# Top-16 cross-attention of a two-layer transformer kernel: its negation moved from GpSimd to ScalarE, one cycle for each tile, scores in four PSUM banks, and the work on tokens at fixed places of the cycle

## What is computed

```
scores = jnp.einsum('bqhd,bkhd->bhqk', q, k) / jnp.sqrt(jnp.float32(D)).astype(h.dtype)
top_s, top_i = jax.lax.top_k(scores, TOPK)
attn = jax.nn.softmax(top_s, axis=-1)
...
o = jnp.einsum('bhqk,bhqkd->bqhd', attn, vg).reshape(B, L, C)
```

## Time and profile before

| | us |
|---|---|
| median of 3 runs (1690.25 to 1695.0) | 1692.53 |
| the profiled execution, its own time | 1693.09 |
| span of its profile | 1691.3 |
| busy in the span: PE / DVE / ACT / POOL | 1469.3 / 917.7 / 694.0 / 385.8 |
| attention 2 in the profile, from the first scores to the last output copy | 207 to 652 |

### The profile page before, as it was taken

One profiled execution on the slowest core, in us unless ns is written; L12 is line 12 of the kernel. 1 busy time (PEld: TensorE's weight loads), 2 busy tenths in 40 slices (PEclk: granted clock), 3 DMA queues, 4 the chain that ended last, 5 costly groups with the idle time before them and its releaser, 6 DMA issues.

```text
span 1691.3 us, 25766 instructions
## 1 busy us (share of the span) xinstructions
PE 1469.3 (87%) x9132; PEld 742.6 (44%) x9132; DVE 917.7 (54%) x2815; ACT 694.0 (41%) x1370; POOL 385.8 (23%) x632
## 2 busy tenths in 40 slices
PE   5999767788887786889899889998999998998898
PEld 3567544454644553343233223333323245453565
DVE  2555467777777766644356655665657335450111
ACT  2255433444344342313435435554455753334211
POOL 0020077775776754000000010000100001010110
PEclk9999967789889887889999989999999999999999
DMA  5022100000000001000010000000000000000000
GB/s 170 1 82 77 49 1 14 7 1 1 4 2 1 27 1 34 0 1 0 1 63 1 1 1 1 1 2 1 1 10 1 1 2 2 11 2 4 14 16 25
DMA packets 22095, 26.77 MB, mean 16 GB/s; under 512 B 4204, under 2 KB 19634, under 8 KB 21708
## 3 DMA queue, kind: packets, MB, share of 16 engines
q1 hardware_dynamic: 21059, 25.03, 4.6%
q10 hardware_dynamic: 909, 0.10, 0.0%
HBM read 21.58 MB, written 3.08 MB: 15 GB/s over the span
## 4 chain that ended last, share of the span: by engine, by line
PE 53%; DVE 6%; ACT 3%; issue 2%; POOL 1%; ACTq 0%; DVEq 0%; POOLq 0%
PE bank L863 24%; PE bank L820 7%; PE bank L901 7%; PE bank L835 5%; PE bank L799 3%; DVE part_max L1294 2%; PE bank L778 2%; PE bank L904 1%; PE bank L906 1%; ACT pr L1087 1%; PE bank L757 1%; DVE x_hat L1267 1%; PE bank L785 1%; ACT h_t L1029 1%; PE bank L764 1%
## 5 line engine op out<-in xcount | busy, mean ns | idle before, releaser
L1087 ACT ACTIVATE pr<-bank 128x512 f32<-128x512 f32 x656 | 355.0, 597 | 440.5 <-PE bank L863 440.5
L1294 DVE TENSOR_REDUCE part_max<-bank 128x1 f32<-128x512 f32 x512 | 328.3, 685 | 269.1 <-PE bank L863 268.2
L863 PE MATMUL bank<-slot 32*128 32x512 f32 (+1 forms) x3072 | 413.2, 530 | 7.8 <-ACT pr L1087 2.8
L863 PEld LDWEIGHTS bank<-slot 32*128 32x128 f32 x3072 | 164.0, 188 | 222.7 <-issue 158.6
L1344 POOL TENSOR_SCALAR var_eps<-mean_var 128x4 f32<-128x4 f32 x24 | 5.4, 227 | 1081.5 <-DVE mean_var L1258 1081.3
L820 PE MATMUL bank<-h_t,w_m 128*128 128x512 f32 x256 | 134.3, 653 | 13.3 <-DVE hidden L1274 7.8
L1104 ACT ACTIVATE exp_all<-bank,neg 128x154 f32<-128x154 f32 x256 | 85.3, 388 | 147.1 <-POOL neg L1389 143.8
L1403 POOL TENSOR_SCALAR left<-left 128x308 f32<-128x308 f32 x128 | 126.1, 985 | 75.7 <-issue 48.4
L901 PE MATMUL bank<-pr,v 128*17 128x512 f32 x1024 | 138.0, 612 | 0.0
L1319 DVE MAX8 top<-bank 128x8 f32<-128x154 f32 x256 | 69.6, 314 | 68.5 <-PE bank L925 65.3
L1406 POOL TENSOR_TENSOR probs<-left,exp_all 128x256 f32<-128x256 f32 x128 | 93.4, 730 | 0.0
(11 more groups left out here) (140 smaller groups left out, 1949.2 us busy)
## 6 DMA issues: line engine op xcount, KB each, us to landing
w_m<-in_L_xcond_w_m SPq DMA_DIRECT2D x1, 2048.0 KB, 9.5
w_m<-in_L_xcond_w_m SPq DMA_DIRECT2D x2, 1024.0 KB, 6.4
w<-in_L_xcond_w SPq DMA_DIRECT2D x2, 1024.0 KB, 6.7
w_ada<-in_L_xcond_w_ada SPq DMA_DIRECT2D x1, 1792.0 KB, 10.2
x_sb<-in_x SPq DMA_DIRECT2D x6, 256.0 KB, 6.7
res_row<-rows_dram SPq DMA_DIRECT2D x12, 128.0 KB, 3.3
out_x<-x_sb SPq DMA_DIRECT2D x6, 256.0 KB, 2.1
wa<-in_L_xcond_w_qkv SPq DMA_DIRECT2D x1, 768.0 KB, 7.3
```

Source lines behind the costliest of these rows:

```text
L863: last = nc.tensor.matmul(g.bank(*tile)[:, into], left, right, start=True, stop=True)
L1087: nc.scalar.activation(m.pr[:, u % NPR, :], g.bank("s", gi, i)[:, :], ACT.Exp).then_inc(g.free("s", gi, i), 1)
L1294: nc.vector.tensor_reduce(m.part_max[:, slot, h * TB + i // 8, i // 4 % 2:i // 4 % 2 + 1], bank[:, :], axis=AX.X, op=ALU.max).then_inc(don ...
```

## The change

Four things are changed, all within attention 2.

1. `c_neg` is issued by ScalarE, as an activation Copy with scale -1.0, and no longer by GpSimd. Its waits stay the same.
2. `topk_run` plans in a cycle of 5.2 us per tile. The scores of a tile are placed about a cycle ahead and rotate over the banks 1, 2, 3, 4. The transposes of a tile stand later, half a cycle into the next tile, and `c_copy` and `c_pv` follow.
3. The dense steps stand at fixed places: once a cycle at 0.35 for stage (2, 1), and at 0.10 and 0.60 of a cycle for (3, 0) and (4, 0), through `under` and `fill`; those that follow on DVE are planned 0.4 of a cycle later. The slots of `gap_slots` put an ACT follow-up right behind its PE step (`ua`, `ua_copy`), and the `silu` of batch 0 come in twos. `joined` lays the head of a block over the tail of the one ahead. The 16 + 45.5 cycles hold the same steps as before.
4. Banks of the dense steps and of `o_turn` of attention 2 are 0 and 6 (bank 6 is shared with `c_tail`; bank 0 is taken first where it is empty), no longer 0 and 1.

The plan of attention 3 begins 0.3 cycles (1.6 us) after the end of attention 2, where it was 3.5 half-tile steps (9.1 us). The number of matmuls, DVE and POOL operations is otherwise the same. The activation tables are loaded for `silu` four times in attention 2 where it was two, with as many loads back to exp.

```diff
     if kind == "c_score":
-        return (2, 3, 4)
+        return (1, 2, 3, 4)
...
     s, b = step[1:3]
-    return (0, 1) if (s, b) in ((2, 1), (3, 0), (4, 0)) else (0, 1, 2)
+    return (0, 6) if (s, b) in ((2, 1), (3, 0), (4, 0)) else (0, 1, 2)
...
+    def fill(self, slots, times, late=0.0):
+
+        assert len(slots) <= len(times), (len(slots), len(times))
+        where = [times[i * len(times) // len(slots)] for i in range(len(slots))]
+        for time, steps in zip(where, slots):
+            for step in steps:
+                self.at(time + late if step[0] in ON_VECTOR else time, step)
+        return where
...
+        tail = [[("ua", s, b, n, j), ("ua_copy", s, b, n, j)] for j in range(HT)]
+        for j in ((HT - 1,) if b else (3, HT - 1)):
+            tail[j] += [("silu", s, b, n, q) for q in range(j // 4 * 2 * (1 - b), (j + 1) // 2)]
+        tail += [[("ub", s, b, n, j), ("hid", s, b, n, j)] for j in range(HT)]
...
 def topk_run(plan, start, step):
...
+                    t0 = start + u * step
+                    plan.at(t0 - 0.75 * step, ("c_score", gi, t, 0), ("c_score", gi, t, 1), ("c_scores", gi, t))
                     for hf in range(2):
...
+                        t1 = t0 + 0.5 * hf * step
+                        plan.at(t1, ("c_top", gi, t, hf))
+                        plan.at(t1 + 0.1 * step, ("c_neg", gi, t, hf))
+                        plan.at(t1 + 0.25 * step, ("c_exp_all", gi, t, hf))
+                        plan.at(t1 + 0.5 * step, ("c_pick", gi, t, hf))
+                    plan.at(t0 + 1.5 * step, ("c_tail", gi, t), ("c_turn", gi, t))
+                    plan.at(t0 + 1.6 * step, ("c_copy", gi, t))
+                    plan.at(t0 + 2.0 * step, ("c_pv", gi, t))
...
-    plan.spread(token_slots(2, 1), A2 + 5, A2 + 37 * step)
...
+    def under(first, last, slots, per=1):
+        return plan.fill(slots, [A2 + (first + (i + 0.5) / per - 0.15) * step for i in range(int((last - first) * per))], 0.4 * step)
+
+    under(1, 17, joined([gap_slots(2, 1, n) for n in range(2)]))
...
+    under(18.5, 64, joined([gap_slots(3, 0, 0), gap_slots(3, 0, 1), gap_slots(4, 0, 0), gap_slots(4, 0, 1)]), 2)
...
-    T = end + 3.5 * step
+    T = end + 0.3 * step
...
+        elif kind == "c_neg":
+            v = plan.order[step]
+            act.wait_ge(m.picked, 4 * v + 2)
+            since(act, (m.all_done, v - 3))
+            nc.scalar.activation(m.neg2[:, v % 4, :], m.top[:, v % 2, :, 0], ACT.Copy, scale=-1.0).then_inc(m.neg_done, 1)
```

More of the change, by code:

```diff
@@ L99, in banks_of @@
     if kind == "o_turn":
-        return (0, 1) if attention(step[1]) == 2 else (0, 1, 2)
+        return (0, 6) if attention(step[1]) == 2 else (0, 1, 2)
     if kind == "down_part":
-        return None if step[4] else banks_of(("y_mm",) + step[1:4])
+        return None if step[4] else (0,) if step[1:3] == (3, 0) else banks_of(("y_mm",) + step[1:4])
     if kind in ("down",) or kind not in RING:
@@ L107, in banks_of, with own_bank @@
     s, b = step[1:3]
-    return (0, 1) if (s, b) in ((2, 1), (3, 0), (4, 0)) else (0, 1, 2)
+    return (0, 6) if (s, b) in ((2, 1), (3, 0), (4, 0)) else (0, 1, 2)
+def own_bank(step):
+    return attention(step[1]) == 2 if step[0] == "o_turn" else step[1:3] in ((2, 1), (3, 0), (4, 0))
+ON_VECTOR = ("x_sum", "stats", "rstd", "x_hat", "hid", "qk_d", "out_sum")
 FOLLOW_UPS = {"v": "v_copy", "ua": "ua_copy", "ub": "hid", "ug": "gelu", "on_turn": "on_copy", "y_mm": "x_sum", "hat_turn": "modulate",
@@ L150, in finish @@
             if banks:
+                banks = [x for x in banks if x not in last or last[x][0] != "down_part" or ("down",) + last[x][1:4] in placed]
                 empty = [x for x in banks if x not in last or follow_up(last[x]) in placed]
-                bank = min(empty or banks, key=lambda x: turn.get(x, -1))
+                first = banks[0] if step[0] in RING and own_bank(step) and banks[0] in empty else None
+                bank = min(empty or banks, key=lambda x: turn.get(x, -1)) if first is None else first
                 if not empty:
@@ L290, in topk_run @@
 def topk_run(plan, start, step):
-    v = 0
+    u = 0
     for b in range(B):
@@ L1384, in gpsimd_program @@
             nc.gpsimd.tensor_tensor(w, w, m.gate_row[:, q % 2, :].unsqueeze(1).to_broadcast([P, HT, C]), ALU.mult).then_inc(m.m2_gated, 1)
-        elif kind == "c_neg":
-            v = plan.order[step]
-            pool.wait_ge(m.picked, 4 * v + 2)
-            since(pool, (m.all_done, v - 3))
-            nc.gpsimd.tensor_scalar(m.neg2[:, v % 4, :], m.top[:, v % 2, :, 0], -1.0, None, ALU.mult).then_inc(m.neg_done, 1)
         elif kind == "c_pick":
```

75 lines of the change are left out of this document (48 added, 27 removed).

## The result

The changed kernel takes 1722.63 us (median of 4 runs, 1721.85 to 1725.8), the kernel before 1692.02 us on the same chip. The ratio is 1.0183, 95% interval 1.0163 to 1.0202: 31 us slower. The forecast was 1637, 55 us faster.

A forecast was written before the change was run, and what follows sets the result against it. It took a loop of GpSimd and ScalarE to bound attention 2. The terms 336 + 21 + 10 + 18 + 8 - 4 = 389 us for 445 gave 1637 us in all, range 1602 to 1675.

The forecast's parts named there:

- The loop of GpSimd and ScalarE: Attention 2: c_pick, negation and exp wait in turn, 3.09 us a half, 6.18 a tile, 395.5 of 445 us.
- The new loop: Attention 2 after the change: c_pick, transposes, copies, negation on ScalarE, exp, next c_pick; 4.8 us a tile.
- What a plain tile costs then: Attention 2: 5.25 us a tile, between DVE's 5.1 and PE's 5.4; 336 us for 64 tiles.
- The check of the sum: Attention 2: 49.5 us beyond the old loop today, kept for the same dense work; 336 + 49.5 = 385 us.
- What the dense steps cost over a plain tile: Attention 2: 21 us for fixed places, 10 for tiles with ub or down in both half-slots, 18 for silus.
- Exp behind the slot: ScalarE, second half-slots: exp waits behind ua_copy and its like, 14 places of 1.5 us, 21; silu bursts before exp, 18.
- Single bank, waits and queues: Bank 0 waits on PE and GpSimd's row and gate_m2 steps: nothing while GpSimd's spare 0.8 us covers; 26 at most.
- The fourth score bank: PE in attention 2: freed to do scores ahead; not priced, between nothing and DVE's idle time, already inside the 336.
- Silus in twos: ScalarE in attention 2: four bursts of 4.5 us, 18 in all; 5.1 us of added table loads.
- Beginning and end: Attention 2: 8 us added before the first transposes, 4 us saved where its last chain no longer holds up PE.
- The slower one: Attention 2: ScalarE and PE wait in turn in every half-slot of (3, 0), (4, 0); 7.5 us a tile, 1736; chance 0.06.
- The clock rival: First 17 tiles of attention 2: TensorE stays at the lower clock, 7.5 us a tile, 38 us lost, 1675; chance 0.20.

The follow-up runs named there:

- e1: The kernel before with only the negation moved to ScalarE; ratio 0.9871 to the kernel before, 22 us faster.
- e2: The changed kernel with the negation back on GpSimd; ratio 1.0292 to the kernel before.
- e18: The changed kernel with the exps alone planned ahead of the dense slots, 0.10 behind the half's start instead of 0.25; ratio 0.9992 to the kernel before.
- e9: The changed kernel with on_copy, modulate and v_copy, the follow-ups of slots with two PE steps, one slot later; ratio 1.0135 to the kernel before.
- e7: The changed kernel without the preference for bank 0, dense steps and output turns in banks 0 and 6 by turns; ratio 1.0114 to the kernel before.
- e3: The changed kernel with the banks of before: scores in 2, 3, 4, dense steps in 0 and 1 by turns; ratio 1.0332 to the kernel before.
- e15: e4 with the banks of before: scores in 2, 3, 4, dense steps in 0 and 1 by turns; ratio 0.9908 to the kernel before.
- e6: The changed kernel with the four silus of a block in one burst; ratio 1.0145 to the kernel before.
- e8: The kernel before with the negation on ScalarE and attention 3 planned 1.6 us after attention 2's end, not 9.1; ratio 0.9852 to the kernel before.
- e4: The changed kernel with dense steps spread as before, banks 0 and 6 by turns; ratio 0.9901 to the kernel before.
- e13: The changed kernel with the dense slots 0.2 of a cycle later, behind exp and scores; ratio 0.9958 to the kernel before.
- e11: e4 with the old cycle of before (old topk_run); ratio 0.9961 to the kernel before.
- e10: The changed kernel with ua_copy, silu and qk_a one slot later, pairs left together; ratio 1.0188 to the kernel before.
- e12: The changed kernel with all ScalarE follow-ups one slot later and banks 0 and 6 by turns; ratio 1.0003 to the kernel before.
- e17: The changed kernel with the scores alone ahead of the dense slots, planned 0.95 of a cycle ahead instead of 0.75; ratio 1.0258 to the kernel before.

## Why the prediction was wrong

**What bounds the kernel: the first step that failed.** The loop of GpSimd and ScalarE was read rightly. Before the change, tiles with none, one or two dense steps all take 6.4 to 6.6 us, near the 6.18 of the loop, and taking the negation away gains 22 us on the kernel before (e1) and 18 on the changed one (e2). The new loop was right too, 4.68 us measured for 4.8. What failed is the next step, "What a plain tile costs then ... 64 x 5.25 = 336 us", a gain of 59.5 us. It put one limit under all 64 tiles. In e1, with the loop gone, tiles with no dense step take 5.84 us, with one 6.00, and the 24 with two stay at 6.58: another limit stood just beneath the loop. The gain is 22 us by e1's ratio, so this term was some 37 us too large. The check of the sum made the same error: it took 49.5 us of disturbances over, though the old loop seems to have hidden most of what the dense steps cost.

**What the dense steps cost over a plain tile: the second step.** It was priced at 21 + 10 + 18 = 49 us. In the same terms the changed kernel has 462.4 - 63 x 5.25 = 132 us. Some 77 of them are there in e1 too, whose dense steps are spread (407.6 - 63 x 5.25); the other 55 belong to the change's order and banks. "About 10 tiles" with two dense steps were to take 6.2 us; there are 19 with two at 8.13 us and 9 with more at 9.87.

**The negation's price.** 0.18 us estimated, 0.207 measured (26.5 us for 128). Near enough.

**Exp behind the slot.** Priced at 21 us for 14 places and 18 for the silus, 39 in all, of which 13 for the silus were there before. Moving exp ahead of the slots gives 32 us (e18), more than the 31 of the whole loss. So the mechanism was seen, and as a sum its size was near. The 14 places are those of second half-slots; 15 more stand in first half-slots and were not priced. And the sum set this cost against a gain of 59.5 us, where the measured gain was 22. The slots with two PE steps or more were priced like the others: moving their follow-ups gave 8 us (e9), and 9.4 us lie between a negation and its exp in the one shown.

**Single bank, waits and queues.** "They cost nothing while that cover holds" is the third step that failed. The preference for bank 0 costs 12 us (e7). The cover was said to be GpSimd's 0.8 us to spare a tile, but these steps hold up PE and ScalarE, and the GpSimd figure says nothing about them.

**The fourth score bank** was put at nothing. With the change's slots, the banks of before (three for scores, 0 and 1 for dense steps) would cost 37 us more (e3 against e7); with dense steps spread, nothing (e15).

**Silus in twos.** 5.1 us of loads by the row; e6 shows 6, with overlapping intervals. It is the timeline that speaks for the row's price and against the drain that the Trainium skill adds. A burst takes 4.6 us where 4.5 was forecast.

**Beginning and end.** -4 us for the end; the time behind the last `c_copy` fell by 9.4. Right in sign, and small. The 8 us of the beginning are hardly the change's: the first `c_copy` is at 225.95 us before and at 227.19 after.

**The rivals.** The slower one had the right place (a follow-up in each half-slot, ScalarE and PE in turn) and 1736 us for the measured 1722.6. It got 0.06 because "only 14 places are of this kind"; with the first half-slots there are 29. The point from which it decides was put at 6.8 us a tile as a mean; the measured mean is 462.4 / 63 = 7.3. That its 1736 lies near is partly luck: it took 7.5 us for every tile, where the measured ones range from 5.7 to 9.9 by kind. The clock rival had stage (2, 1) as its place, and there the first 17 tiles took 107.5 us, 109.3 before. The clock isn't quite out as a contributor: PE was busy 13.7 us longer for the same matmuls, and no run holds the clock fixed, so how much of the 31 us went through it stays open.

**The signs.** Of those named beforehand, the wait of exp for the negation went, and the forecast loop and silu bursts are there. Attention 2 at 485 us (370 to 410 forecast), the "issue" idle of the mask at 100.4 us and a clock of 0.81, not above 0.82, said that the sum was wrong.

A tally, in us against the kernel before: negation and earlier end -25 (e8); the new cycle and the new banks, with dense steps spread, +8 (from e8 to e4); the placing of the dense steps +48 (from e4 to the changed kernel). That makes the measured +31. The forecast had -59.5 for the loop and +3.5 for all the rest. Of the 48, moving the slots behind the exps gives back 38 (e13), exp's own place 32 (e18) and banks by turns 12 (e7); these overlap, and don't add. Of the 8, e11 gives 18 for the banks in the old cycle and e15 nothing in the new one, so how they are split stays open.

## What to carry to other kernels

When a small operation is taken out of a loop that bounds a stretch, sort the tiles by what else they hold and ask for each kind what bounds it once the loop is gone. The mean tells nothing of that: here tiles with two dense steps had another limit at the same 6.58 us, hidden under the loop. When side work is given a fixed place in a cycle of in-order engines, look at which operation that others wait for comes right behind it (here exp). In this kernel, moving the slots by 0.2 of a cycle was worth 38 us with their contents unchanged, and moving exp alone 32. The version that beats both kernels is the kernel before with only the negation moved, 0.9871, or 0.9852 with attention 3 planned earlier.

## What the runs showed that I had not expected

Delays of this kind don't add: follow-ups one slot later gave 8 us for one half of them and nothing for the other, banks by turns 12, and all together 30 (e9, e10, e7, e12). A part of this may be the planner, which moves follow-ups forward again where a bank is short: an edit of planned times has to be read in the order that comes out of it. Bringing the scores forward, which looks like a way to feed DVE earlier and nothing else, made the kernel 13 us slower (e17). And the same choice of banks is worth 37 us under one order of steps, 18 the other way under another, and nothing under a third (e3 against e7, e11 against e8, e15 against e4).
